# Relation counts turned by transposing transfers instead of TensorE, and a block's four low one-hots interleaved

## The reference

```
x = layernorm(x + gcn_batchnorm_gelu(x))              # sums over edges, degree-normalised
x = layernorm(x + two_sage_layers(x))                 # means over edges, two weights each
x = layernorm(x + two_rgcn_gate_layers(x))            # two relations: each edge has type 0 or 1,
                                                      #   w_r = sum_b att[r,b] * basis[b], 30 bases
x = layernorm(x + relu((x + sum_over_edges(x)) W1 + b1) W2 + b2)
```

## Time and profile before

| | us |
|---|---|
| median of three runs | 917.75 |
| the profiled execution's own time | 917.2 |
| its span on the core (what the profile shows) | 915.4 |
| TensorE busy | 882.8 (96%) |
| VectorE busy | 656.2 (72%) |
| ScalarE busy | 280.8 (31%) |
| counting, up to the first dense product | 0 to 184.6 |

### The profile page before, as it was taken

How to read it: one execution, slowest core, us unless ns; L and a number is a source line. 1 busy time by engine, 2 the same in 40 slices (tenths; PEclk the granted TensorE clock), 3 DMA queues, 4 the chain that set the end, 5 groups by cost and what they waited for, 6 DMA issues and landing times.

```text
span 915.4 us, 12673 instructions
## 1 busy us (share of the span) xinstructions
PE 882.8 (96%) x4258; PEld 428.2 (47%) x4258; DVE 656.2 (72%) x1286; ACT 280.8 (31%) x431; POOL 87.9 (10%) x66
## 2 busy tenths in 40 slices
PE   7999999999959999899997999999999999999997
PEld 3555555554545444344443444444444444444443
DVE  6898978658987797998999988975324255552247
ACT  0333444637752116222312111114311221132221
POOL 1000111301220003021210000003200020020000
PEclk9999999999979999999998999999999999999999
DMA  8955665596435885788464655530131014322228
GB/s 275 352 168 165 183 188 191 149 238 198 155 95 157 200 236 150 208 207 204 128 150 108 155 141 161 139 91 1 35 81 23 12 47 139 82 62 41 47 60 237
DMA packets 134888, 129.50 MB, mean 141 GB/s; under 512 B 80687, under 2 KB 81156, under 8 KB 134826
## 3 DMA queue, kind: packets, MB, share of 16 engines
q10 hardware_dynamic: 96192, 60.25, 26.1%
q1 hardware_dynamic: 38634, 68.45, 24.9%
HBM read 97.80 MB, written 12.52 MB: 121 GB/s over the span
## 4 chain that ended last, share of the span: by engine, by line
PE 68%; DVE 15%; DMA 8%; ACT 4%; issue 2%; POOL 1%; DVEq 1%; ACTq 0%; SPq 0%
PE Dp L696 25%; PE Dp L666 24%; PE T L620 11%; PE Dp L572 6%; DVE acc L1262 4%; DMA stage<-in_basis 3%; DMA wst<-mixd 2%; DMA xr<-xres 2%; DVE Zraw L1373 1%; ACT W L1010 1%; DVE stt L1354 1%; ACT wst L863 1%; DVE w L1391 1%; PE T L666 1%; POOL Zraw L530 1%
## 5 line engine op out<-in xcount | busy, mean ns | idle before, releaser
L666 PE MATMUL Dp<-W,hT 128*128 128x512 f16 x792 | 175.7, 381 | 3.6 <-DMA hT<-S 3.6
L696 PE MATMUL Dp<-Zraw,A 128*128 128x512 f16 x800 | 173.0, 379 | 0.0
L1262 DVE SCALAR_TENSOR_TENSOR acc<-stage,att,acc 128x512 f32<-128x512 f32 x232 | 163.5, 770 | 4.3 <-DMA stage<-in_basis 4.3
L696 PE MATMUL Dp<-Zraw,AT 128*128 128x512 f16 x600 | 130.0, 379 | 0.0
L666 PEld LDWEIGHTS Dp<-W,hT 128*128 128x128 f16 x792 | 77.8, 98 | 96.6 <-DMA hT<-S 3.8
L696 PEld LDWEIGHTS Dp<-Zraw,A 128*128 128x128 f16 x800 | 78.2, 98 | 94.4
L696 PEld LDWEIGHTS Dp<-Zraw,AT 128*128 128x128 f16 x600 | 58.7, 98 | 70.8
L1140 DVE TENSOR_SCALAR Zraw<-hT,w 128x640 f16<-128x640 f16 (+1 forms) x209 | 85.9, 456 | 0.3
L1391 DVE SCALAR_TENSOR_TENSOR w<-Dp,aggc,S 128x512 f32<-128x512 f32 x40 | 29.9, 747 | 59.9 <-PE Dp L696 54.0
L962 ACT ACTIVATE Zraw<-Dp,zsc 128x512 f16<-128x512 f32 x46 | 29.4, 684 | 125.8 <-PE Dp L666 121.7
L620 PE MATMUL T<-stage,W 128*128 128x512 f32 x120 | 60.5, 627 | 5.5 <-DMA stage<-in_basis 5.5
(11 more groups left out here) (176 smaller groups left out, 950.4 us busy)
## 6 DMA issues: line engine op xcount, KB each, us to landing
stage<-in_basis SPq DMA_DIRECT2D x180, 256.0 KB, 2.9
Zraw<-in_basis SPq DMA_DIRECT2D x60, 256.0 KB, 3.1
xres<-w ACTq DMA_DIRECT2D x30, 256.0 KB, 2.3
xr<-xres ACTq DMA_DIRECT2D x30, 256.0 KB, 3.1
wst<-in_Wn ACTq DMA_DIRECT2D x4, 1024.0 KB, 5.6
wst<-in_Ws ACTq DMA_DIRECT2D x4, 1024.0 KB, 6.0
wst<-mixd ACTq DMA_DIRECT2D x4, 1024.0 KB, 6.0
wst<-in_root ACTq DMA_DIRECT2D x3, 1024.0 KB, 6.7
```

The source lines that it names most:

```text
L666: last = nc.tensor.matmul(dense_bank(u, t, m), turned[:, hp, k * P:(k + 1) * P], weights_of(u, m)[:, wp, k, :], start=(n == 0), stop=(n == ...
L696: last = nc.tensor.matmul(sum_bank(t), a[:, k, ds(t * P, P)], Z[:, r, h, k, :], start=(n == 0), stop=(n == count - 1))
L1262: last = v.scalar_tensor_tensor(part, stage[:, q, :], a, part, ALU.mult, ALU.add)
```

## The change

1. `turn_counts`, `turned_out`, `count_bank`, `COUNT_STEPS` and their semaphores are gone. In their place ScalarE issues two transposing transfers per tile, one per relation, 128x1280 fp16 each, straight from B to A (`move_counts`), behind the fourth window of the tile. B's free condition is now the landing of these transfers.
2. B is laid out relation first (`p j r s c` for `p j s r c`), and the keys are formed to match.
3. The four lows of a window's fixed chunks are interleaved: column k of chunk c stands at 4k + c. A new constant `iota_c` (each number four times, 512 columns, made by POOL) lets `lows_of` read and write with step 1. TensorE reads such a low as weights with a column step of four elements. The lows of the loop's chunks stay packed.
4. TensorE and VectorE wait for all of the transposing transfers before B's place is written again, and before `A` is read.

```diff
-        B = zview(...).rearrange("p (j s r c) -> p j s r c", j=2, s=NT, r=REL)
+        B = zview(...).rearrange("p (j r s c) -> p j r s c", j=2, s=NT, r=REL)
...
+            pool.iota(iota_c, [[1, P], [0, 2 * FIXED]], base=0, channel_multiplier=0, **kw).then_inc(s_const, 1)
...
             def chunk_product(slot, j, start=False, stop=False):
+                if isinstance(slot, int):
+                    n = 2 * FIXED
+                    four = slot // n * n
+                    low = oh_lo[:, four * P:(four + n) * P].rearrange("p (k c) -> p k c", c=n)[:, :, slot % n]
+                else:
+                    low = oh_lo[:, ds(slot * P, P)]
                 for b in range(2):
-                    last = nc.tensor.matmul(Dp[:, j, b, 0:HALF], oh_lo[:, ds(slot * P, P)],
+                    last = nc.tensor.matmul(Dp[:, j, b, 0:HALF], low,
...
-            def turn_counts(t, g, bank):
-                pe.wait_ge(s_wev, PER * (t + 1))
-                for r in range(REL):
-                    for i in range(2):
-                        last = nc.tensor.matmul(bank[:, ...], B[:, t % 2, 2 * g + i, r, :],
-                                                ident[:, :], start=True, stop=True)
-                last.then_inc(s_at, 1)
...
             for w in range(NWIN):
                 window(w, w % 2)
                 t = w // PER - 1
                 if t >= 0:
-                    for g in COUNT_STEPS[w % PER]:
-                        wait(pe, s_ate, 5 * t + g - 1)
-                        turn_counts(t, g, count_bank(t, g))
                     if w % PER == 2:
                         degrees(t)
                 mix(mix_share(w))
-            pe.wait_ge(s_ate, 5 * (NT - 1))
             pe.wait_ge(s_mxe, GROUPS)
...
                     if u == 0 and t == 0:
                         degrees(NT - 1)
-                        for g in range(3):
-                            turn_counts(NT - 1, g, LAST_BANKS[g])
-                    if u == 0 and t == 2:
-                        for g in range(3, 5):
-                            pe.wait_ge(s_ate, 5 * (NT - 1) + g - 2)
-                            turn_counts(NT - 1, g, LAST_BANKS[g - 3])
...
             def window_out(w):
                 if t > 1 and w % PER == 0:
-                    act.wait_ge(s_ate, 5 * (t - 1))
+                    act.wait_ge(s_moved[t % 2], 16 * len(MOVED) * (t // 2))
...
-            def turned_out(t, g, bank):
-                act.wait_ge(s_at, t * 5 + (g + 1))
-                nc.scalar.activation(A[:, :, t, 2 * g * P:2 * (g + 1) * P], bank...., ACT.Copy).then_inc(s_ate, 1)
+            def move_counts(t):
+                act.wait_ge(s_wev, PER * (t + 1))
+                for r in MOVED:
+                    act.dma_start_transpose(A[:, r, t, :].rearrange("p (s n) -> p s n", s=NT),
+                                            B[:, t % 2, r, :, :].rearrange("p s c -> p (s c)")).then_inc(s_moved[t % 2], 16)
...
                     window_out(w)
-                    if t:
-                        for g in COUNT_STEPS[i]:
-                            turned_out(t - 1, g, count_bank(t - 1, g))
                     if w == NWIN - 1:
                         turn_to(4, 0)
+                    if i == PER - 1:
+                        move_counts(t)
                     for g in range(groups_done(w - 1) if w else 1, groups_done(w)):
                         mixed_out(g)
...
             def lows_of(slot, c):
                 n = 2 * FIXED
-                v.tensor_tensor(oh_lo[...].rearrange("p (c k) -> p c k", c=n),
-                                iota_n[:, 0:P].rearrange("p (c k) -> p c k", c=1).broadcast_to([P, n, P]),
-                                lo_h[:, ds(c, n)].rearrange("p (c k) -> p c k", k=1).broadcast_to([P, n, P]), ALU.is_equal)
+                v.tensor_tensor(oh_lo[...].rearrange("p (k c) -> p k c", c=n),
+                                iota_c.rearrange("p (k c) -> p k c", c=n),
+                                lo_h[:, ds(c, n)].rearrange("p (k c) -> p k c", k=1).broadcast_to([P, P, n]), ALU.is_equal)
```

More of the change, by code:

```diff
@@ L31 @@
 HALF = KEYS // 2
-COUNT_STEPS = ((0,), (1, 2), (3,), (4,))
+MOVED = (0, 1)
 MIX_FIRST = 3
@@ L148, in resnorm_gnn_kernel @@
         dstr = hview(4 * 2 * P).bitcast(i32).rearrange("p (g e) -> p g e", g=2)
+        iota_c = dstr.bitcast(f16).rearrange("p g e -> p (g e)")
         wlo = hview(4 * NWIN).bitcast(f32)
@@ L213, in resnorm_gnn_kernel @@
         s_wev = sem("s_wev")
-        s_at = sem("s_at")
-        s_ate = sem("s_ate")
+        s_moved = [sem(f"s_moved{j}") for j in range(2)]
         s_xin, s_xmax, s_s0 = sem("s_xin"), sem("s_xmax"), sem("s_s0")
@@ L224, in resnorm_gnn_kernel @@
         e_att = sem("e_att")
-        s_eye, s_mixT = sem("s_eye"), sem("s_mixT")
+        s_mixT = sem("s_mixT")
         mx_full = [sem(f"mx_full{i}") for i in range(MIX_SLOTS)]
@@ L265, in resnorm_gnn_kernel @@
         s_xst = {u: [sem(f"s_xst{u}_{j}") for j in range(2)] for u in LN}
-        b_idf, b_one, b_dg, b_row, b_rev = (sem("b_" + n) for n in ("idf", "one", "dg", "row", "rev"))
+        b_one, b_dg, b_row, b_rev = (sem("b_" + n) for n in ("one", "dg", "row", "rev"))
         b_ev, b_st, b_mv, b_sd, b_co, b_g = (sem("b_" + n) for n in ("ev", "st", "mv", "sd", "co", "g"))
@@ L431, in resnorm_gnn_kernel @@
         XS_FROM = 19
-        Z_SCALED = 38
+        Z_SCALED = 39
         def halves_split(u):
@@ L590, in window @@
                 pair_product(FIXED * (w % 2) + 1, j, stop=True).then_inc(s_win, 1)
-            def turn_counts(t, g, bank):
-                pe.wait_ge(s_wev, PER * (t + 1))
-                for r in range(REL):
-                    for i in range(2):
-                        last = nc.tensor.matmul(bank[:, (2 * r + i) * P:(2 * r + i + 1) * P], B[:, t % 2, 2 * g + i, r, :],
-                                                ident[:, :], start=True, stop=True)
-                last.then_inc(s_at, 1)
             def degrees(t):
@@ L624, in _ @@
             mix(PAIRS)
-            pe.wait_ge(s_const, 10)
+            pe.wait_ge(s_const, 11)
             pe.wait_ge(s_tbl, 1)
@@ L688, in agg @@
                         pe.wait_ge(s_own[u], NT - 1 + SUM_BANK[t][0])
+                    if u == 3 and t == 0:
+                        for i in range(2):
+                            pe.wait_ge(s_moved[i], 16 * len(MOVED) * NT // 2)
                     rels = [(A[:, r], r) for r in range(REL)] if nz == 2 else [(AT, 0)]
@@ L903, in _ @@
                 weight_work("counts", 0, t)
-            act.wait_ge(s_const, 10)
+            act.wait_ge(s_const, 11)
             nc.scalar.activation(sd[:, 0:1], epsc[:, :], ACT.Sqrt)
@@ L980, in first_z @@
                     z_out(t, j)
-                    if u == 0 and t in (0, 2):
-                        for g in range(3) if t == 0 else range(3, 5):
-                            turned_out(NT - 1, g, LAST_BANKS[g % 3])
                     if u == 0 and t == 6:
@@ L1087, in _ @@
             dve.wait_ge(s_const, 8)
[L1088 to L1089 removed]
+            link(v.tensor_tensor(eye, ident[:, 0:P // 2], ident[:, P // 2:P], ALU.add))
             def mix_table(a0, a1):
@@ L1113, in _ @@
             v.tensor_scalar(src_i, src_i, P - 1, None, ALU.bitwise_and)
-            link(v.tensor_copy(key_f, typ_i))
+            link(v.tensor_scalar(key_f, typ_i, float(NT), None, ALU.mult))
             v.tensor_copy(lo_f, src_i)
@@ L1135, in _ @@
             dve.wait_ge(s_tbl, 1)
-            dve.wait_ge(s_const, 8)
+            dve.wait_ge(s_const, 9)
             def key_of(w, slot, c):
@@ L1314, in _ @@
                 dve.wait_ge(s_mxst[j], 16 * REL * GROUPS // 2)
-            v.tensor_copy(identf, ident[:, :]).then_inc(b_idf, 1)
-            dve.wait_ge(b_idf, 1)
+            link(v.tensor_copy(identf, ident[:, :]))
             for t in range(NT):
@@ L1482, in _ @@
                     dve.wait_ge(s_bn, 48)
+                    for i in range(2):
+                        dve.wait_ge(s_moved[i], 16 * len(MOVED) * NT // 2)
                     weight_work("agg", 0, 0)
```

19 lines of the change are left out of this document (5 added, 14 removed).

## The result

| | before | after |
|---|---|---|
| median, us | 917.87 (916.77 to 920.0, 4 runs) | 928.46 (928.0 to 930.35, 4 runs) |
| ratio to before, as recorded | | 1.0123, 95% interval 1.0105 to 1.014 (the two medians give 1.0115) |
| profiled execution, us | 917.2 | 928.0 |
| its span, us | 915.4 | 926.2 |
| start of tile 9's degrees matmuls (TensorE), us | 187.16 | 198.60 |

The account below looks back on a forecast made before the run. TensorE was taken to bound the counting, with VectorE close behind; -9.5 (groups) + 0.5 (evacuations) + 5.3 (last window) - 1.1 (dense products) = -4.8 us against 917.2 gave 912.4 us, range 907.5 to 921.

Parts of the forecast that it names:

- Turned groups, -9.5 and -1.1: Removing TensorE's count-turning groups saves 9.5 us up to window 39's end and 1.1 us in the dense products.
- The lows, 437 ns: VectorE's interleaved low of four chunks takes 437 ns instead of 690, a gain of 0.25 us per window.
- The step of four, 0: In TensorE's window matmuls, loading weights with a column step of four stays hidden and costs 0 us.
- Rival D: The stepped weight load shows in TensorE's window matmuls: at 196 ns, +19.2 us, total 931.6 us; chance 0.10.
- POOL's added iota ... costs nothing: At the start, POOL's iota lies behind an all-reduce ending 4 us before VectorE's first low, and costs nothing.
- One of 128x1280 is issued in 1.56 us by size, two in 3.1 us: ScalarE's issue time for a tile's transposing transfers, scaled from 1.25 us for 128x1024; 3.1 us hides behind window evacuations.
- rival E: ScalarE's slow issues block its stream in every tile; at b = 8.4 for a pair, +10.3 us, 927.5 us; chance 0.08.
- That is 0.5 us each; the one at window 11 vanishes: Mix-group evacuations behind the transfers at windows 11 and 23 delay TensorE 0.5 us each; window 11's vanishes; term +0.5 us.
- I take b = 5.5: +5.3 us: At the last window, b, the issue time of two large transfers, delays the first dense product: 5.5 us, costing +5.3 us.
- B: Last window: large transfers go out before SP's loads are felt, b = 3.1, +2.9 us; total 910.0 us; chance 0.12.
- C: VectorE's low does not become faster in the counting, saving 7.1 instead of 9.5 us; total 914.8 us; chance 0.14.
- F: The gain is given back behind the dense products, where 10 us load waits do not move; 917 us; chance 0.06.

Follow-up runs that it names:

- g4: f1 with one wait more: POOL's subtraction for the first weights' low halves starts only after VectorE's last key; no transfers; 913.56 us, ratio 0.9948.
- f1: f0 without the 20 transposing transfers, A filled by ScalarE in unit 3 with copies of AT (wrong counts); 914.42 us, ratio 0.9965.
- g3: Kernel before with the interleaved lows and the column step of four alone, their constant made by VectorE; 916.13 us, ratio 0.9975.
- f0: Changed kernel with the constant of the lows made by VectorE, nothing added to POOL; 929.19 us, ratio 1.0121.
- f3: f0 with half the columns of every mix input loaded from the 9th on, so mixed weights are wrong; 919.99 us, ratio 1.0029.
- g1: f0 with a mix group's evacuation put ahead of the two transposing transfers, which stay pairs; 921.96 us, ratio 1.0043.
- e1: Changed kernel with POOL's new iota put ahead of its all-reduce instead of behind it; 931.26 us, ratio 1.0148.
- f2: f0 with a tile's two transfers issued apart, behind later windows' evacuations (tile 9's behind dense tiles 6 and 8); 921.03 us, ratio 1.0007.
- e2: Kernel before with the interleaved lows, the column step of four and POOL's iota ahead of its all-reduce; 917.22 us, ratio 0.9995.
- g2: Kernel before with interleaved lows, VectorE's constant, and transposing pairs behind evacuations for tiles 2 to 8 only; TensorE turns the others; 913.51 us, ratio 0.9947.

## Why the prediction was wrong, point by point

**The balance.** At tile 9's degrees the forecast was -9.5 + 0.5 + 5.3 = -3.7 us, and +11.4 was measured. The saving came within 0.4 us. The costs were put at 5.8 us and came to 20.5: ahead of window 38's degrees 10.1 instead of 0.5, in the tail 10.4 instead of 5.3. So the step that failed is the price of ScalarE's issues, first in the early tiles, where it was put at 3.1 us for a pair at all times, then in the last one.

**Turned groups, -9.5 and -1.1: right.** g4 has no turned groups and no transfers and is 9.1 us ahead at tile 9's degrees; the dense products give another 1.1. The collision of f1, which takes 4 us of this when nothing else delays the counting, has no term in the prediction.

**The lows, 437 ns: right.** The first takes 0.42 us, the whole group 498 ns in the mean where it was 713, a gain of 215 ns (250 forecast). The group of the counting in the kernel after, with TensorE's weight loads:

```profile
L574 PEld LDWEIGHTS Dp<-Zraw 128*128 128x128 f16 x320 | 35.8, 114 | 32.7 <-issue 21.5 <-ACT Zraw L750 3.6 <-DVE Zraw L1121 1.9
...
L1132 DVE TENSOR_TENSOR Zraw<-hT,Zraw 128x512 f16<-128x512 f16 x40 | 19.9, 498 | 28.1 <-issue 14.4 <-PE Dp L574 12.5 <-DVE i_in L1262 0.9
...
L574 PEld LDWEIGHTS Dp<-Zraw 128*128 x98 | 9.6, 98 | 4.6 <-issue 1.4
```

**The step of four, 0: right.** The load went from 98 to 114 ns and stays under the 136 ns that hide it; the loads with an address from a register, which are packed still, take 98 ns in the same trace. Ten matmuls still take 1.36 us in the chain, and g3, with the step, is 0.25% faster than before. Rival D falls: the doubled load of 196 ns, which the Trainium skill's rule on fast loads (TensorE: Matmul & The Clock Gate, Fast Weight Load and DoubleRow) would have given if taken strictly, is not there. The Trainium skill's note on cachelines (SBUF — State Buffer), by which this step is free, agrees better: 16 ns more for a load, none for the matmuls.

**"POOL's added iota ... costs nothing": wrong.** The step looked at the all-reduce and VectorE's low, not at POOL's change from one to the other: 8.09 us pass between them, and the low comes 5.0 us later. Behind window 6, after the waits there, 1.9 us against g4 are left of it (45.11 and 43.23). It is not the cause of the result: f0, without it, is no faster than after (1.0121 and 1.0123). Its start 4.4 us earlier is lost again behind its first pair.

**"One of 128x1280 is issued in 1.56 us by size, two in 3.1 us": wrong where it matters.** In the calm middle a pair takes 3.4 to 3.6 us, close to the forecast. But the pairs for tiles 0, 1 and 2 took 5.37, 9.53 and 7.69 us. The prediction took its row for one moment (181 us) as the price at all times, with 0.89 of share up to 55 us standing in the earlier trace rows and named under rival E. With the transfers the share rose from 0.60 to 1.15 between 55 and 76 us, where +0.2 was forecast; that work which had been late piles up there is likely, but not shown. f3 shows that the other loads are the cause: with half of them the first three pairs fall from f0's 11.51, 5.22 and 3.45 us to 4.73, 3.53 and 3.06. Why the same pair takes 5.37 us in one kernel and 11.51 in another with the same loads is not shown.

**"That is 0.5 us each; the one at window 11 vanishes": the wrong place.** E's own formula, b - 3.5 at window 11, gives 4.2 us with the measured b of 7.7; measured 5.28, and 2.0 us more for the four mix products behind the gap at the lower clock, a price that no term has. Behind window 7 not even a window's evacuation hid: it came at 59.12, and TensorE waited 0.88 us. At window 23 it is 1.12 us. By window 22, 1.1 us of it were recovered.

**"I take b = 5.5: +5.3 us": the mechanism right, the size off.** b was 7.8, near the upper end of 8.4. ScalarE came to window 39's evacuation 0.65 us late, at 182.66, behind tile 8's pair and the work on the weights, and TensorE's first dense products took 4.76 instead of 2.75 us. 7.8 + 0.65 + 2.0 = 10.45 against the 10.4 by which this piece is longer than in g4. The last term had no place in the prediction: in the 9.30 us of idle time the granted clock falls to 0.50 and stays there up to 198 us, so the gap costs its own length and then the slower products. Behind g1's gap of 1.48 us the granted clock is 1.00.

**Rivals.** E is what happened, but in the first three tiles and the last, not in every one: 927.5 forecast, 928.0 measured, at a chance of 0.08. Its sum came close partly by luck: window 23 cost 1.1 us where it had 5.8 and window 28 nothing where it had 2.0, while the clock, the waits for evacuations of windows and the late start are in none of its terms. B (cheap tail), C (lows not faster) and D fall; F too, since all that is lost is lost by 224 us.

## What to carry to other kernels

The issue of a transposing transfer is work in the stream of the engine that issues it, and it is longer where many other loads are under way: price it at the busiest stretch it will stand in, and put nothing behind it that another engine needs within that time. Work taken off the engine that bounds is worth what it weighed (9 us here) only if what replaces it is kept out of the stretches that are full already: replacing it in seven of ten tiles gave a gain of 0.5%, of which the interleaved lows alone are 0.25%; in all ten it was a loss of 0.4% with the mix group's evacuation ahead of the pair (g1) and of 1.2% behind it.

## What the runs showed of the hardware

- In the kernel after, an issue of 320 KB took from 1.35 to 6.4 us (median 2.09) on ScalarE, and landed after 5.0 to 16.4 us.
- The twenty transfers took the queue from 26.1% of 915.4 us to 30.2% of 926.2 on all 16 engines: 40.8 us, 2.0 us for each, where 1.4 was forecast from the earlier trace rows. That is 160 GB/s (an estimate from 327,680 bytes). Part of it is crowding: the other queue, with the same packets, rose from 24.9% to 25.5%, 8 us more. The Trainium skill (Advanced Engine Details and Errata, X-Bar Transpose (TRN2)) has transposing transfers as fast as regular ones; here the stretch from 20 to 55 us, where no large transposing transfer is issued, moved 303 GB/s at a share of 0.89, 340 at full share and twice as fast, and the quiet stretch with transposing transfers alone moved 55 GB/s at 0.28, 196 at full share, so the trace doesn't agree. The queues, with packets, MB and share, before:

```profile
q10 hardware_dynamic: 96192, 60.25, 26.1%
```

after:

```profile
q10 hardware_dynamic: 122432, 66.80, 30.2%
```

- POOL is idle for 8.09 us from an all-reduce to an iota (after), and for 6.13 to 7.58 us ahead of an all-reduce that follows its other work (after, e1), in the kernel before too (6.79).
- Still open: why f2 scatters over 15 us; by what path other loads lengthen an issue, and why the first pairs differ so much between kernels with the same loads; why e2's profiled execution loses 5 us in unit 2; what makes the pair of g2 at 115.63 us take 6.64 us when the two ahead of it took 3.4. Whether a second engine could issue these transfers was not tried.
